# Moving the scratch of a quantizer from SBUF to two idle PSUM banks, in a fused attention and FP4 feed-forward kernel

## The reference

```python
def fp4_quant_dequant(x):
    xb = x.reshape(shape[:-1] + (shape[-1] // BLOCK, BLOCK))
    scale = jnp.max(jnp.abs(xb), axis=-1, keepdims=True) / 6.0
    scale = jnp.maximum(scale, jnp.float32(1e-12))
    xn = xb / scale
    idx = jnp.searchsorted(_MID, jnp.abs(xn))
    q = _GRID[idx] * jnp.sign(xn) * scale
    return q.reshape(shape)
...
gate = fp4_linear(x, w_gate)
y = fp4_linear(x, w_up)
h = jax.nn.silu(gate) * y
return fp4_linear(h, w_down)
...
x = x + _L0_attn_ref(_layernorm(x, axis=-1), ...)
x = x + _L0_ffn_ref(_layernorm(x, axis=-1), ...)
```

## Time and profile before

| what | us |
|---|---|
| median of the timed runs (2 runs, 10380.33 to 10388.84) | 10384.59 |
| the profiled execution, whole | 10394.81 |
| its span, slowest core (core 0) | 10393.0 |
| spans of the eight cores | 10350.5 to 10393.0 |
| VectorE busy in it | 5762.8 (55%) |
| TensorE busy in it | 4118.7 (40%) |
| ScalarE busy in it | 1476.9 (14%) |

### The profile page before, as it was taken

The page is one execution under the profiler, slowest core; times in us unless marked ns, Lnnn a source line. Parts: engine busy times, 40 slices in busy tenths (PEclk is TensorE's granted clock), DMA queues, the critical chain, the costliest instruction groups (busy, mean ns, idle before and its releaser), DMA issues.

```text
span 10393.0 us, 61061 instructions; the slowest of 8 cores (10350.5 to 10393.0 us)
## 1 busy us (share of the span) xinstructions
PE 4118.7 (40%) x18304; PEld 1751.7 (17%) x18304; DVE 5762.8 (55%) x6821; ACT 1476.9 (14%) x2262; POOL 239.4 (2%) x445
## 2 busy tenths in 40 slices
PE   0000354555554555541334433533343334333433
PEld 0000122222222222220112111211111112111211
DVE  8999434444344443343574457445744574457445
ACT  0000223223222323220000000000000000000000
POOL 0000000000000000000000000000000000000000
PEclk9999966666666666665667666767676767776767
DMA  3111111111111111114101110111011101110111
GB/s 73 46 43 58 41 46 46 41 39 47 44 46 44 39 39 48 46 34 85 35 17 37 37 38 16 37 37 32 20 40 37 30 24 38 37 35 19 37 37 31
DMA packets 547589, 408.86 MB, mean 39 GB/s; under 512 B 479424, under 2 KB 479424, under 8 KB 546240
## 3 DMA queue, kind: packets, MB, share of 16 engines
q1 hardware_dynamic: 495392, 215.66, 8.4%
q0 software_dynamic: 51872, 189.30, 4.9%
HBM read 118.56 MB, written 180.88 MB: 29 GB/s over the span
## 4 chain that ended last, share of the span: by engine, by line
DVE 47%; DMA 17%; PE 16%; DVEq 6%; issue 6%; SPq 6%; ACT 2%; ACTq 0%; POOLq 0%; PEldq 0%; POOL 0%
DVE bfar L283 10%; DVE bfar L276 10%; DMA bfar<-hqs 9%; DVE far L259 3%; DVEq L287 3%; PE ps L669 3%; PE ps L548 3%; DVE bfar L292 3%; DVE bfar L272 3%; PE ps L502 2%; DVE far L270 2%; DVE far L267 2%; DMA hqs<-bfar 2%; PE ps L557 2%; DVE bfar L841 2%
## 5 line engine op out<-in xcount | busy, mean ns | idle before, releaser
L502 PE MATMUL ps<-bfar 128*128 128x512 bf16 x3072 | 838.6, 444 | 2288.2 <-DMA bfar<-xn1s 1893.0
L827 PE MATMUL ps<-bfar 128*128 128x512 bf16 (+1 forms) x3072 | 763.1, 418 | 1323.8 <-ACT bfar L816 1323.8
L889 PE MATMUL ps<-bfar 128*128 128x512 bf16 x2816 | 727.7, 408 | 1231.1 <-DMA bfar<-hqs 1230.8
L804 PE MATMUL ps<-bfar 128*128 128x512 bf16 (+1 forms) x3072 | 755.6, 415 | 931.3 <-DMA bfar<-xqs 702.6
L283 DVE SCALAR_TENSOR_TENSOR bfar<-far,bfar 128x1024 bf16<-128x1024 f32 (+1 forms) x768 | 872.7, 1136 | 60.1 <-issue 3.4
L502 PEld LDWEIGHTS ps<-bfar 128*128 128x128 bf16 x3072 | 334.9, 110 | 2791.2 <-issue 2604.0
L909 DVE TENSOR_TENSOR far<-far,ps 128x1024 f32<-128x1024 f32 x64 | 78.2, 1221 | 1272.4 <-PE ps L889 1094.9
L841 DVE TENSOR_TENSOR bfar<-ps,bfar 128x2816 bf16<-128x2816 f32 x64 | 197.9, 3092 | 995.4 <-PE ps L827 795.8
L276 DVE SCALAR_TENSOR_TENSOR bfar<-far,bfar 128x1024 bf16<-128x1024 f32 (+1 forms) x576 | 654.5, 1136 | 45.0 <-issue 2.6
L283 DVE SCALAR_TENSOR_TENSOR bfar<-ps,bfar 128x1024 bf16<-128x1024 f32 (+1 forms) x464 | 628.1, 1354 | 36.1 <-issue 1.7
L252 ACT ACTIVATE bfar<-bfar 128x1024 bf16<-128x1024 bf16 (+1 forms) x192 | 189.1, 985 | 3169.7 <-DVE bfar L292 2078.5
(11 more groups left out here) (72 smaller groups left out, 4446.5 us busy)
## 6 DMA issues: line engine op xcount, KB each, us to landing
hqs<-bfar POOLq DMA_DIRECT2D x64, 704.0 KB, 3.4
far<-x SPq DMA_DIRECT2D x64, 512.0 KB, 5.6
x1s<-far POOLq DMA_DIRECT2D x64, 512.0 KB, 2.9
far<-x1s SPq DMA_DIRECT2D x64, 512.0 KB, 6.5
out<-far POOLq DMA_DIRECT2D x64, 512.0 KB, 2.9
xn1s<-bfar POOLq DMA_DIRECT2D x64, 256.0 KB, 2.3
aos<-bfar POOLq DMA_DIRECT2D x64, 256.0 KB, 2.3
xqs<-bfar POOLq DMA_DIRECT2D x64, 256.0 KB, 2.3
```

The source lines that it names most:

```text
L502: last = e.matmul(ps[:, col:col + 512], lhs_fn(k), rhs_fn(k), start=(k == 0), stop=(k == 7))
L804: last = e.matmul(ps[:, ns:ns + nw], bfv(F_XQT + k * CHUNK + t * 128, [[1, 128]]), bfv(WGQ + k * FI + ns, [[1, nw]]), start=(k == 0), stop ...
L827: last = e.matmul(ps[:, ns:ns + nw], bfv(F_XQT + k * CHUNK + t * 128, [[1, 128]]), bfv(WUQ + k * FI + ns, [[1, nw]]), start=(k == 0), stop ...
L889: last = e.matmul(ps[:, PS_DN + t * DM + half * 512: PS_DN + t * DM + half * 512 + 512], bfv(F_HQT + sl * 512 + t * 128, [[1, 128]]), bfv( ...
```

## The change

The three quantizations of every tile in phase 2 get their scratch `u` in PSUM, from column 3072 on (`PS_QU`), in place of `far`. These are banks 6 and 7; the gate and up products use banks 0 to 5 only. The down product uses all eight banks, so its first matmul now waits for the VectorE count after the last quantization, `sV.n`, in place of the one after the last multiplication. Phases 0 and 1 are as they were.

```diff
@@ -848,7 +848,7 @@
                         bfv(F_H + qoff, [[1, Fs]]),
                         bfv(F_H + qoff, [[16, Fs // 16], [1, 16]]),
                         bfv(F_H + qoff, [[16, Fs // 16], [1, 16]]),
-                        Fs, usb=X_SB + 4096 + 2048, nboff=qoff // 16)
+                        Fs, uoff=PS_QU, nboff=qoff // 16)
                 sG.take(16)
 
                 def st(e, t=t, vq=qdone, tguard=lhqt_last[0]):
@@ -860,7 +860,7 @@
                 p.on("gpsimd", st)
 
             hq_done = sG.n
-            vlast = vh_inc[0]
+            vlast = sV.n
             dn_pe = []
             for cc in range(22):
                 sl = cc % 4
```

## The result

| what | us |
|---|---|
| kernel before, median of 8 runs | 10384.59 (10359.77 to 10403.54) |
| changed kernel, median of 9 runs | 10488.86 (10464.87 to 10498.4) |
| ratio, with its 95% interval | 1.0097 (1.0084 to 1.0110) |
| span of the profiled execution | 10466.6 (core 2; all cores 10444.3 to 10466.6) |

The change costs 104 us by the medians; the ratio, 0.97%, makes it 101. The forecast was 96. The interval (87 to 114 us) excludes no change by a wide margin.

The account below looks back on a forecast made before the run. VectorE's quantization was taken to bound phase 2, with no slack. 1505 ns per tile over 64 tiles gives 96 us, 93.4 of it L272; 10384.6 + 96 = 10481 us, 0.9% slower, range 10446 to 10532.

Parts of the forecast that it names:

- which edit costs: Phase 2 quantizations: L272 loses its fast form (531 and 398 ns), L267 and L270 take 8 and 7 ns more; 96 us.
- all of it on the path: Phase 2: all four quantizations of a chunk delay the run in full, 1505 ns per tile over 64 tiles.
- The lead of the up product: Before L841 in phase 2: the up product is done 1.7 us before L841 starts, growing to 2.1 us.
- The new wait costs nothing: First down matmul: its wait for the last quantization is met before its existing wait for the transposed load; no cost.
- the fixed extra for each PSUM instruction: Rival: all 1920 PSUM-touching instructions pay extra; from 60 ns each 10593 us, by the skill's 65 ns 10602; chance 2%.
- The clock rival: Gate and up products on TensorE stay at the 1.2 GHz level after longer gaps: some 10910 us; chance 1.5%.
- The surviving fast form: Rival: L272 still takes 694 and 560 ns out of PSUM, leaving 3 us: 10387 us; chance 1%.
- hidden work: Rival: the up product ends last and covers quantizations of tiles 1 to 3: 10409 us at the least; chance 2.5%.

Follow-up runs that it names:

- The doubled comparison: Kernel before with the comparison L272 done twice in phase 2, scratch in SBUF: 10524.59 us against 10384.06, ratio 1.0147.
- tile 3 alone: Kernel before with the scratch in PSUM only for tile 3 of each chunk, first down matmul waiting for the last quantization: 10406.77 us against 10384.73, ratio 1.0022.
- the new wait alone: Kernel before, scratch still in SBUF, but the first down matmul waits for the last quantization: 10391.67 us against 10384.06, ratio 1.0012.
- the last experiment: Kernel before with the scratch moved to SBUF in phases 0 and 1 too: 10333.21 us against 10384.73, ratio 0.9949.
- The slow-form run: Kernel before, scratch in SBUF, with phase 2's comparison L272 written with two tensor inputs: 10475.2 us, ratio 1.0098.
- the unchanged kernel: Kernel before with no edit, timed again as if it were another: 10402.88 us against 10400.26, ratio 0.9999.

## Why the prediction was right

The step "which edit costs" held in every row. L272 lost its fast form for exactly the 531 and 398 ns of the forecast; 958 ns for the 768 form, which had no row and was taken from a line through two widths, was met to the nanosecond. The 8 and 7 ns of L267 and L270 came as 8 and 7, and at 768 columns as 9 and 8 (967 against 958 and 959). The sum, 96 us, is the growth of VectorE's busy time to 0.4 us.

The step "all of it on the path" was the risky one, since a busy time is no run time. The doubled comparison (140.5 us for 140) and tile 3 alone (22 for 24) show it by dose, each within some 20 us or less, and the unchanged wait for the store shows it in the profile. The lead of the up product, forecast to grow by 0.41 us, grew by 0.25 in the profile (gate waits 4.76 to 5.01 us). It moves with TensorE's clock by more than that: in the one execution of the new wait alone these 48 waits came to 205.4 us on core 2 (granted clock 0.701) and to 235.9 on core 4 (0.722). It decided nothing.

"The new wait costs nothing" held as far as the timing can tell.

One sentence was too cautious: that a measurement of this kernel tells about 2% from no change. The interval of the comparison is 0.26% wide, and it puts a loss of half that mark clear of noise.

Of the rivals, the fixed extra for each PSUM instruction is ruled out for these forms: 0 ns on L283 at both widths and 7 to 9 on a write, where it would have needed 60. The table of the Trainium skill ("VectorE: DVE Perf Modes", the section on the TRN2 errata) prices reads of PSUM that write SBUF, and would have given 65 ns for each; the forecast's 124 us stretched it to L267 and L270 too, which write PSUM. It does not hold here: the two-operand forms have the same duration from either memory, and a line through two widths leaves L272 a fixed part of 161 ns from SBUF (694 and 1627 ns, the second from the last experiment) and 158 out of PSUM (1225 and 3092). The clock rival did not come: no wait of L841 in tiles 1 to 3 ended on the up product, and the profiled core's mean clock was 0.718 after and 0.712 before. The surviving fast form is ruled out by 128 and 64 slow instances, hidden work by the experiments.

The same skill page says, in its section "Why PSUM operands drop a tier", that f32 out of PSUM is processed at one element per cycle. The rows agree: (3092 - 1225) ns / 1792 columns is 1.04 ns for a column from PSUM, one cycle at the 0.96 GHz that the forecast took from that page, and (1627 - 694) / 1792 is 0.52 from SBUF. The slow-form run adds that an instruction with a second tensor operand is as slow within SBUF.

The medians moved by 104 us, 8 more than the sum. The interval, 87 to 114 us, holds 96, and nothing here shows a cause for the rest. It may be no more than the scatter of the runs.

## What to carry to other kernels

Price a move of a buffer form by form and not by memory: here nine of ten instructions cost nothing to 9 ns, and one took 1.7 to 1.8 times as long, the only one with a single tensor operand and a faster form to lose. When VectorE bounds a stage, keep an f32 buffer that a single-operand instruction reads in SBUF, even where idle PSUM banks look free. Before comparing two profiled spans, check the waits on all cores: a difference of 25 us sat in one core's wait for one product.

## What was not expected

In one and the same execution the cores of a kernel differ by about half of the effect that was studied. Spans and granted clocks of the run with the new wait alone:

```profile
core 2: 10406.7 us, clock 0.701
core 3: 10400.7 us, clock 0.702
core 4: 10350.0 us, clock 0.722
core 5: 10360.0 us, clock 0.721
```

The slowest core sets the time. Here the slow cores are those with the lower granted clock, 41 to 57 us behind, and most of that before phase 2 (first L841 at 4910.4 us on core 2 and at 4865.2 on core 4). But the clock is not all of it. In the profile of the unchanged kernel two cores with nearly the same clock lie 49 us apart:

```profile
core 4: 10414.5 us, clock 0.700
core 5: 10365.6 us, clock 0.702
```

Of these 49 us, 26.5 are in one wait, that of L909 for the down product (1094.5 against 1068.0 us), the same oddity as on core 0 of the kernel before; its cause was not looked for. Such scatter goes into the slowest core's time whatever the kernel, and limits how small an effect these medians can show.
